# A decoder layer with a two-level Kronecker mixture of experts: the first down products spread over four quadrants, the offsets sent by a small transfer, one GELU form, and a new order of steps for all turns

## What is computed

```
n = layernorm(x)
k, v, q = fft(n Wk' + bk), fft(n Wv' + bv), fft(n Wq' + bq)
s = cumsum(k * v over the sequence) * conj(q)
x = x + real(ifft(s / (1e-9 + |s|))) / 16
x = x + cross attention(layernorm(x), ctx)         # 16 heads of 64, causal, ALiBi slopes
t = layernorm(x) seen as 64 tokens of 1024 = 32 x 32
h = gelu(kmoe(t, up)); x = x + kmoe(h, down)
kmoe: logits = t W'; top 2 of 64 experts, softmax over the two;
      out = sum over the two of p * (A[e] @ token @ B[e]')   # up 32x32 -> 64x64, down 64x64 -> 32x32
```

## Time and profile before

| | |
|---|---|
| three runs, median | 1326.86 us |
| profiled execution | 1330.54 us |
| its span, first to last instruction | 1328.8 us |
| mean granted TensorE clock | 0.981 |
| instructions | 52143 |
| start of `wo` of batch 0, 1, 14, 15 | 93.05, 161.17, 1155.58, 1232.26 us |

### The profile page before, as it was taken

The page is one execution under the profiler, slowest core; times in us unless marked ns, Lnnn a source line. Parts: engine busy times, 40 slices in busy tenths (PEclk is TensorE's granted clock), DMA queues, the critical chain, the costliest instruction groups (busy, mean ns, idle before and its releaser), DMA issues.

```text
span 1328.8 us, 52143 instructions
## 1 busy us (share of the span) xinstructions
PE 1227.9 (92%) x16626; PEld 985.8 (74%) x16626; DVE 965.7 (73%) x3677; ACT 1086.9 (82%) x3158; POOL 594.2 (45%) x1846
## 2 busy tenths in 40 slices
PE   7999999999999999999999999999999989987785
PEld 5677787877778787777778777777877777775574
DVE  1466778695978879596877969587786959777554
ACT  2557898898988899898889989798888979888654
POOL 3112446262645536363544636354553625453242
PEclk9999999999999999999999999999999999999798
DMA  9200101010110101010010101001010100101000
GB/s 287 49 17 14 38 10 42 11 42 19 30 31 13 40 14 41 16 37 24 18 39 14 42 11 41 19 19 42 11 42 12 41 19 19 34 13 32 4 25 10
DMA packets 66210, 42.58 MB, mean 32 GB/s; under 512 B 18065, under 2 KB 64786, under 8 KB 65682
## 3 DMA queue, kind: packets, MB, share of 16 engines
q1 hardware_dynamic: 65938, 39.25, 10.7%
HBM read 34.98 MB, written 4.19 MB: 29 GB/s over the span
## 4 chain that ended last, share of the span: by engine, by line
PE 54%; DVE 16%; issue 10%; SPq 10%; ACT 2%; POOL 2%; DMA 2%; DVEq 1%; POOLq 0%; ACTq 0%
SPq L483 9%; PE P L809 5%; PE X L869 5%; PE P L786 4%; PE P L775 4%; PE PT L869 4%; PE PT L832 4%; PE P L762 3%; DVE own L1142 3%; PE F L949 3%; PE X L856 3%; DVE chosen_dn L423 3%; PE S L825 2%; DVE probs L1101 2%; PE G L908 2%
## 5 line engine op out<-in xcount | busy, mean ns | idle before, releaser
L423 POOL COPY chosen_dn<-experts 64x64 f32 x1000 | 222.5, 279 | 214.2 <-issue 146.4
L664 ACT ACTIVATE probs<-probs,neg_max 128x128 f32<-128x128 f32 (+1 forms) x512 | 226.5, 444 | 24.0 <-DVE neg_max L1101 20.7
L409 POOL COPY chosen_up<-experts 32x128 f32 x512 | 182.3, 356 | 116.5 <-POOL chosen_up L409 49.7
L409 ACT COPY chosen_up<-experts 32x128 f32 x528 | 156.0, 296 | 15.5 <-PE G L955 6.2
L1101 DVE CUSTOM_DVE_ANT_0 probs<-S,distance 128x128 f32<-128x128 f32 (+1 forms) x512 | 151.9, 351 | 12.9 <-PE S L825 9.4
L832 PE MATMUL PT<-ident,probs 128*128 128x128 f32 x768 | 135.8, 286 | 10.3 <-DVE probs L1119 7.2
L703 ACT ACTIVATE hT<-h 64x1024 f32<-64x1024 f32 x64 | 127.0, 1984 | 11.3 <-DVE h L1232 9.9
L1119 DVE TENSOR_TENSOR probs<-probs,rinv 128x768 f32<-128x768 f32 x128 | 129.1, 1009 | 4.4
L775 PE MATMUL P<-ctxT,wk 128*128 128x256 f32 x512 | 124.5, 388 | 2.1 <-DVE x L1079 2.1
L786 PE MATMUL P<-wv,ctxT 128*128 128x256 f32 x512 | 122.5, 382 | 0.0
L1108 DVE COPY probsT<-PT 128x384 f32<-128x384 f32 x128 | 71.3, 557 | 70.0 <-PE PT L832 68.8
(11 more groups left out here) (133 smaller groups left out, 2855.2 us busy)
## 6 DMA issues: line engine op xcount, KB each, us to landing
chosen_up<-in_experts_up SPq DMA_DIRECT2D x992, 16.0 KB, 1.7
x<-in_x SPq DMA_DIRECT2D x16, 256.0 KB, 2.7
ctxT<-in_ctxT SPq DMA_DIRECT2D x16, 256.0 KB, 3.3
out<-x2b SPq DMA_DIRECT2D x16, 256.0 KB, 2.3
experts<-in_experts_up SPq DMA_DIRECT2D x2, 1024.0 KB, 19.8
wk<-in_xWk SPq DMA_DIRECT2D x1, 1024.0 KB
wo<-in_xWo SPq DMA_DIRECT2D x1, 1024.0 KB
wv<-in_xWv SPq DMA_DIRECT2D x1, 1024.0 KB, 7.7
```

The costliest lines, as they stand in the source:

```text
L409: last = copy(to[row:row + D1, n * 2 * F1:(n + 1) * 2 * F1], experts_up[k][:, bass.ds(held[g % loaded(units), unit], 2 * F1)])
L423: last = copy(dst, src.rearrange("p (m c) -> p m c", m=2))
L664: act.activation(probs[:, e % 4, lo:hi], probs[:, e % 4, lo:hi], ACT.Exp, bias=neg_max[:, e % 4, rt:rt + 1], scale=-1.0, accum_out=rsum[:, ...
```

## The change

- **Four quadrants.** `dn_first` alternates between the two groups of a pair: the group j = 0 goes to `F` as before, the group j = 1 to `G`, with the halves of the output crossed. For that the experts of odd groups are copied with their two matrices in different row halves, by two copies instead of one. `dn_weigh` becomes two operations, one from `F` and one from `G`. `dn_second` and `y_keep` use a bank of the `P` pair.
- **Addresses.** `place` is an integer tile of 64x2; a DMA on SP (`send_up`, `send_dn`) writes it into the row `offsets`. The diagonal and the product that spreads it hold the shares alone (128 columns). The casts are gone; the choosers load their registers from strided views.
- **One activation.** GELU is applied once, in place; then two copies on ScalarE and two on GpSimd write `hT`.
- **Order.** A new `ORDER`; 19 turns, all by it. `DRAIN`, `LAST_CHOOSERS` and `warm` are gone.

The diff, cut to its core:

```diff
-LAST_CHOOSERS = {...}
-P_USERS = ("turn1", "f", "inverse", "turn2", "k", "v", "q")
+P_USERS = ("turn1", "f", "inverse", "turn2", "k", "v", "q", "dn_second")
-G_USERS = ("logits_up", "spread_up", "up", "router_dn", "spread_dn", "dn_second", "y_turn")
+G_USERS = ("logits_up", "spread_up", "up", "router_dn", "spread_dn", "dn_first", "y_turn")
-    for turn in range(BATCH + 1):
+    last = max(lag for _, _, lag in order)
+    for turn in range(BATCH + last):
         for name, n, lag in order:
             if 0 <= turn - lag < BATCH:
                 yield name, n, turn - lag
-    for word in DRAIN.split():
...
-        SPREAD = 2 * TOKENS * TOPK
+        SPREAD = TOKENS * TOPK
...
+        def hT_parts(half, oh):
+            src = h[half * F1:(half + 1) * F1, :].rearrange("p (n h o) -> p h o n", h=2, o=F1 // 2)[:, oh]
+            return hT[oh * F1:(oh + 1) * F1, :, half * TOKENS // 2:(half + 1) * TOKENS // 2], src
...
         def choose_dn(copy, held, i, units):
-            to = chosen_dn[i % DN_SLOTS]
+            to, flip = chosen_dn[i % DN_SLOTS], i % 2
...
+                if flip:
+                    copy(to[(1 - half) * F1:(2 - half) * F1, a:a + D1], experts_dn[:, bass.ds(held[i % loaded(units), unit], D1)])
+                    last = copy(to[half * F1:(half + 1) * F1, b:b + D1],
+                                experts_dn[:, D1:][:, bass.ds(held[i % loaded(units), unit], D1)])
+                    continue
...
+            def send(c, layer):
+                groups = (UP_GROUPS, DN_GROUPS)[layer]
+                sp.wait_ge(route_step[layer], at(c, 4, 1))
+                for name in choosers_of(("up", "dn")[layer]):
+                    if name != "sync":
+                        after(sp, chosen[name][layer], at(c, groups, 0))
+                to = offsets[layer][:, :].rearrange("p (n k) -> p n k", k=TOPK)
+                sp.dma_start(to, place[layer][:, :]).then_inc(offsets_ready[layer], 16)
...
+            def turn_tokens(c):
+                after(pool, parts_done, c)
+                pool.wait_ge(h_ready, at(c, 2, 2))
+                for oh in range(2):
+                    pool.tensor_copy(*hT_parts(1, oh)).then_inc(hT_pooled, 1)
+                pool.wait_ge(hT_pooled, at(c, 2, 2))
...
             def gelu(c):
                 wait_g(act, "up", UP_PAIRS, c)
-                after(act, parts_done, c)
-                for half in range(2):
-                    for oh in range(2):
...
-                        act.activation(dst, src, ACT.Gelu).then_inc(hT_ready, 1)
                 cols = UP_PAIRS // 2 * UP_TOK * F1
-                act.wait_ge(hT_ready, at(c, 4, 4))
                 for i in range(2):
                     part = slice(i * cols, (i + 1) * cols)
                     act.activation(h[:, part], h[:, part], ACT.Gelu).then_inc(h_ready, 1)
+            def turn_tokens(c):
+                after(act, parts_done, c)
+                act.wait_ge(h_ready, at(c, 2, 2))
+                for oh in range(2):
+                    act.copy(*hT_parts(0, oh)).then_inc(hT_ready, 1)
...
-                pe.matmul(G[:, 128:384], route_ones[:, :], route_diag[layer][:, :], start=True, stop=True).then_inc(route_spread[layer], 1)
+                pe.matmul(G[:, 128:256], route_ones[:, :], route_diag[layer][:, :], start=True, stop=True).then_inc(route_spread[layer], 1)
...
-                for j in (0, 1):
-                    g, slot = i + j * DN_PAIRS, (2 * i + j) % DN_SLOTS
-                    for u in range(DN_TOK // 2):
+                for u in range(DN_TOK // 2):
+                    for j in (0, 1):
+                        g, slot = i + j * DN_PAIRS, (2 * i + j) % DN_SLOTS
+                        token, one = g * UP_TOK + u, slice((j * 4 + u) * w, (j * 4 + u + 1) * w)
                         for half in range(2):
-                            rows = slice(half * F1, (half + 1) * F1)
-                            token = g * UP_TOK + u
-                            mm = pe.matmul(F[rows, (j * 4 + u) * w:(j * 4 + u + 1) * w], h[rows, token * F1:(token + 1) * F1],
+                            rows, to = [slice(e * F1, (e + 1) * F1) for e in (half, half ^ j)]
+                            mm = pe.matmul((F, G)[j][to, one], h[rows, token * F1:(token + 1) * F1],
...
-                dve.tensor_tensor(W_dn[:, :].rearrange("p (s w) -> p s w", w=D1),
-                                  F[:, :].rearrange("p (s w) -> p s w", w=D1),
-                                  spread(pm[1][:, i * n:(i + 1) * n], 2, D1), ALU.mult).then_inc(f_kept, 1)
+                for j, (bank, kept) in enumerate(((F, f_kept), (G, g_kept))):
+                    part, by = slice(j * n * F1 // 4, (j + 1) * n * F1 // 4), slice(i * n + j * n // 2, i * n + (j + 1) * n // 2)
+                    dve.tensor_tensor(W_dn[:, part].rearrange("p (s w) -> p s w", w=D1),
...
```

More of the change, by code:

```diff
@@ L85 @@
-scale.0@1 gap_up@2 q_keep.2@1 turn1 choose_dve.18@3 weights_up@2 turn_a.0@1 choose_act.17@3 score.1@1 q_keep.3@1
-catch_a.0@1 dn_first.0@3 turn_b.0@1 mask.1@1 choose_act.18@3 choose_act.19@3 spread_up@2 v.0@1 dn_weigh.0@3 keep_up@2
-choose_sync.0@2 xnT1 dn_second.0@3 exp.1@1 catch_b.0@1 choose_dve.19@3 score.2@1 dn_first.1@3 v_keep.0@1 scale.1@1
-pv.0@1 y_keep.0@3 mask.2@1 dn_weigh.1@3 choose_sync.1@2 choose_sync.2@2 choose_act.0@2 choose_sync.3@2
-choose_pool.20@3 choose_act.20@3 choose_act.21@3 choose_act.1@2 turn_a.1@1 choose_dve.20@3 f.0 dn_second.1@3
@@ L90 @@
-choose_act.2@2 score.3@1 exp.2@1 choose_act.3@2 choose_dve.21@3 choose_pool.21@3 dn_first.2@3 y_keep.1@3
-choose_dve.22@3 scale.2@1 dn_weigh.2@3 catch_a.1@1 f_keep.0 keep_out.0@1 choose_pool.22@3 choose_act.4@2
-choose_act.22@3 choose_dve.23@3 f.1 turn_b.1@1 catch_b.1@1 mask.3@1 choose_sync.4@2 choose_sync.5@2 choose_sync.6@2
-choose_sync.7@2 f_keep.1 v.1@1 turn_a.2@1 pv.1@1 choose_pool.23@3 dn_second.2@3 choose_act.23@3 choose_pool.0@2
-own_dve@2 exp.3@1 dn_first.3@3 score.4@1 y_keep.2@3 catch_a.2@1 turn_b.2@1 catch_b.2@1 dn_weigh.3@3 keep_out.1@1
@@ L95 @@
-v_keep.1@1 v.2@1 scale.3@1 dn_second.3@3 pv.2@1 choose_pool.1@2 turn_a.3@1 y_keep.3@3 mask.4@1 choose_pool.2@2
-y_turn@3 choose_pool.3@2 own_act@2 choose_pool.4@2 final@3 store@3 choose_pool.5@2 v_keep.2@1 catch_a.3@1 exp.4@1
-v.3@1 turn_b.3@1 cross.0 product_kv keep_out.2@1 lane.0 up.0@2 catch_b.3@1 weigh.0@2 score.5@1 up.1@2 choose_act.5@2
-choose_act.6@2 choose_act.7@2 scale.4@1 mask.5@1
-"""
-DRAIN = """
-pre.0@14 pv.3@15 turn_a.4@15 catch_a.4@15 keep_out.3@15 weigh.1@14 turn_b.4@15 catch_b.4@15 score.6@15 mask.6@15
@@ L142 @@
[L142 to L158 removed]
+choose_pool.3@3 choose_pool.4@3 k.1@1 spread_up@3 turn_b.3@2 keep_up@3 up.0@3 mask.5@2 weigh.0@3 k_keep.1@1
@@ new lines @@
+weigh.6@3 turn_a.7@2 catch_a.7@2 mask.0@1 q.2@1 pre.5@3 turn_b.7@2 choose_sync.15@3 up.7@3 catch_b.7@2 pv.7@2 pre.6@3
+weigh.7@3 ln1_root ln1 q_keep.1@1 score.1@1 up.8@3 exp.0@1 keep_out.7@2 pre.7@3 gelu@3 hT_pool@3 wo.0@2 wo.1@2
+hT_act@3 router_dn@3 logits_dn.0@3 mask.1@1 q_keep.2@1 scale.0@1 exp.1@1 x2.0@2 x2.1@2 ln3_stats@2 ln3_root@2
+x1_bias@1 logits_dn.1@3 logits_dn.2@3 logits_dn.3@3 part@3 fold@3 top_dn@3 send_dn@3 choose_pool.16@3 ln3@2 gap_dn@3
+v.1@1 scale.1@1 weights_dn@3 q.3@1 v_keep.1@1 choose_dve.16@3 turn_a.0@1 spread_dn@3 ln3_turn@2 choose_dve.17@3
@@ new lines @@
+keep_dn@3 choose_pool.17@3 choose_act.16@3 catch_a.0@1 ln3_keep@2 turn1 turn_b.0@1 choose_pool.18@3 catch_b.0@1
+choose_dve.18@3 score.2@1 mask.2@1 logits_up@2 pv.0@1 top_up@2 own_dve@2 choose_dve.19@3 send_up@2 xnT1 q_keep.3@1
+choose_act.17@3 exp.2@1 turn_a.1@1 v.2@1 v_keep.2@1 dn_first.0@3 choose_act.18@3 choose_pool.19@3 keep_out.0@1
+catch_a.1@1 f.0 f.1 turn_b.1@1 choose_act.0@2 f_keep.0 dn_weigh.0@3 scale.2@1 catch_b.1@1 choose_act.19@3
+dn_second.0@3 choose_pool.20@3 f_keep.1 dn_first.1@3 score.3@1 choose_act.20@3 gap_up@2 choose_act.1@2 dn_weigh.1@3
@@ new lines @@
+pv.1@1 dn_second.1@3 choose_sync.0@2 choose_sync.1@2 choose_pool.21@3 choose_pool.22@3 y_keep.0@3 choose_act.2@2
+choose_dve.20@3 turn_a.2@1 f.2 choose_act.3@2 choose_act.21@3 choose_sync.2@2 y_keep.1@3 choose_act.4@2 f_keep.2
+choose_dve.21@3 mask.3@1 choose_dve.22@3 v.3@1 catch_a.2@1 exp.3@1 choose_pool.23@3 cross.0 dn_first.2@3 score.4@1
+choose_sync.3@2 product_kv lane.0 turn_b.2@1 k.3@1 v_keep.3@1 dn_weigh.2@3 keep_out.1@1 choose_dve.23@3 catch_b.2@1
+mask.4@1 load_ctx dn_second.2@3 choose_act.22@3 choose_act.23@3 pv.2@1 k_keep.3@1 dn_first.3@3 score.5@1 scale.3@1
@@ L978, in dn_second @@
             def dn_second(c, i):
-                take_g("dn_second", i, c)
+                bank = take_p("dn_second", i, c)
                 wait_f(pe, "dn_first", i, c)
+                wait_g(pe, "dn_first", i, c)
                 for odd in (0, 1):
```

219 lines of the change are left out of this document (76 added, 143 removed).

## The result

The changed kernel takes **1447.1 us** (median of four runs, 1444.8 to 1448.3), the kernel before 1326.4 on the same chip. The ratio is **1.091 (1.089 to 1.093)**: 121 us slower, where 10 us less were forecast. The profiled execution's span is 1446.5 us against 1328.8.

A forecast was written before the change was run, and what follows sets the result against it. TensorE's own work was taken to bound the steady turns, a chain of dependent steps the last two stretches. Turns -22, start +5, before the last wo -9, behind it +16 gave -10 on 1328.8, carried over to 1316 us; range 1297 to 1340.

The forecast's parts named there:

- Part 1(a): Odd down groups: one 64x64 copy becomes two; GpSimd half copy 0.15 us, odd group 2.4 (1.5 to 3.0), off TensorE.
- Part 2: Offsets by small transfer: spreading products save 0.5 us a batch, transfer takes 2.0, GpSimd's doubled down-offset loads 2 x 0.57.
- Part 3: One GELU, then strided copies, 2.6 us each on GpSimd: TensorE waits 1.7 us a turn at the router (0.2 to 3.9).
- rival 1: The router's wait on TensorE isn't absorbed: a turn becomes 77.1 us, total 1347, slower; chance 0.24.
- Part 1: Four-quadrant first down products: a dn_first step falls from 1.04 to 0.63 us, saving 1.6 us a batch on TensorE.
- Rival 3: In dn_first the four quadrants don't overlap: the saving falls to 0.5 us a turn, total 1340; chance 0.04.
- Part 4: The steady turn between wo starts: from 76.5 to 74.8 us (73.4 to 77.9), -22 us over 13 turns.
- Part 5: Both ends: start +5 us, before the last wo -9, behind the last wo +16 (8 to 24).

The follow-up runs named there:

- a1: The changed kernel with odd groups' copies made one row half after the other instead of alternating, four quadrants kept: 1358.7 us, ratio 1.028.
- b5: The kernel before with odd down groups chosen by two 64x32 copies into the same row half, nothing crossed: 1364.1 us, ratio 1.027.
- a5: The changed kernel with odd groups' copies made one row half after the other and up offsets packed side by side: 1341.7 us, ratio 1.011.
- a4: The changed kernel with the crossing undone (first down products in two quadrants) and up offsets packed side by side: 1339.4 us, ratio 1.013.
- a2: The changed kernel with GpSimd's and ScalarE's up offsets sent again, packed so that register loads read eight neighbouring values: 1426.1 us, ratio 1.079.
- b3: The kernel before with its steady order run for 19 turns, without written-out end, last-batch shares and filler products: 1344.2 us, ratio 1.012.

## Why the prediction was wrong

**The step that failed first: Part 1(a), the price of a half copy.** I took 0.15 us, from the elements, and bounded an odd group by 1.5 and 3.0 us. A half copy that changes the row half costs 0.25 us on GpSimd, an odd group 4.0, outside my bounds. I scaled a row of another pattern: the eight copies of the earlier trace rows all write the same rows. I laid this cost off TensorE, so in the sum for the turn it stood at nothing; TensorE waited 50 us for these copies over the 13 turns, and their order was worth 5.8 us a turn (a1).

**The same step also lacked cover.** I wrote that the price lies off TensorE and let it lie beside other work. In the earlier trace rows `dn_first` starts without a wait, and I didn't ask how much slack the copies had before the product needed them. The rows had the answer: GpSimd's second group ends at 565.06 and the product starts at 565.85. Over the turns the last copy ended 0.8, 0.5, 0.8 and 1.9 us (medians) before the four products of a batch, while each odd group grew by 2.5 us. b5 gives the price in the old order, 2.1 us a turn for the added copies even at the cheap rate, the larger part of it not in `dn_first` but in what VectorE makes behind its copies. In the new order a5 against a4 shows the same in small: TensorE saves 1.7 us and the turn 0.2.

**Part 2, the loads.** I counted the down loads' doubling (2 x 0.57, the median of a row in which up and down loads are mixed; measured 4 x 1.08 in place of two of 2.0) and missed the up loads altogether. Offsets laid out by the small transfer put gaps between the pairs, and a load goes from 0.57 to 1.88 us. It is worth 1.5 us a turn (a2). The transfer itself lands in 1.7 us at the median; I had taken 2.0. The transfer has landed before `choose_dve.16`, as I said. But VectorE is idle there 1.16 us in each turn, for its two loads of 0.6 us each, where it was mostly 0.49. `keep_dn` stands behind it, and the up router waits for `keep_dn`: 12.0 us over the 13 turns (line 866 above), where it waited 1.0.

**Part 3 and rival 1, the router's wait: not there.** One copy on GpSimd takes 1.95 us; I took 2.6, about the middle between 2.0 and 3.4, and 0.5 for interference. The strided ScalarE row was the right neighbour and the two-operand row the wrong one. The bounds of the wait, 0.2 and 3.9, don't follow from 2.0 and 3.4 either: with the stated terms they are 0 (without interference) and 3.3, and 0 is what came. ScalarE's strided copy takes 2.0 us, as its strided GELU did. (The rule on throughput that I drew from the Trainium skill, "ScalarE: Activation LUTs", stands there under "Step-by-step: what each stage is for".) The Trainium skill, "GPSIMD Engine Reference" (7. Performance pitfalls for Q7 kernels), states about 2.9 cycles an element for strided reads, which gives 2.5 us here, an estimate; the trace disagrees, 1.95 us, and the measurement decides. Rival 1 said slower, and slower it is, but by another wait: its price was 8 us in the turns and its place was the router. A rival about the copies was missing, since I had bounded them too tightly.

**Part 1, the products: right, and better.** A `dn_first` step runs from 610.41 to the next step's start at 610.90, 0.49 us; I took 0.63 where it was 1.04. The step's first line stands in the section on the result; these are its last line and the next step:

```profile
610.89 0.22 PE L945 MATMUL G<-chosen_dn,h 64*64 64x64 f32 x2
610.90 0.43 PE L792 MATMUL S<-kT,qT 64*64 64x128 f32 x8
```

It is the four quadrants and not the second bank: a4, which writes both banks from two quadrants, takes 1.08 us from its first product to the next step.

```profile
640.46 0.33 PE L953 MATMUL F<-chosen_dn,h 64*64 64x64 f32 x4
...
641.54 3.72 PE L740 MATMUL P<-xnT,wf 128*128 128x256 f32 x16
```

Four such steps save 2.2 us a batch, and TensorE's busy time with the copies grouped (a5) is 71.6 us a turn after 73.5. Rival 3 falls. The bracket in the step's first line shows what took the saving: 1.37 us of waiting, in one step of four.

**Part 4, the turn.** Forecast 74.8, measured 82.8. Of the 8.0 us, the alternation is 5.8 (a1), the strided up loads 1.2 to 1.5 (a5 against a1, a2 against the changed kernel), and about 1.0 stays when both are gone (a5, 75.8): there TensorE is idle 4.2 us a turn, where it was 3.0 before.

**Part 5, the ends.** Start +5: right. Behind the last `wo`: the old order with the common end gives +19 for +16 (b3), in the pieces that I had named, so the mechanism was right; the changed kernel shows +31. The last `pre` starts 76.5 us behind `wo` where I had 70 (`store` of batch 14 is issued at 49 instead of 43), and from the last `place` to the end it takes 39 us where I had 29. With the crossing gone and loads packed (a4) these are 68 and 32. Before the last `wo` I forecast 68; a1, a4 and a5 show 72 to 73. The work moved out of that turn was less than the 9 us I took off; that size is off in every variant.

**Small slips in the sums.** The median 1326.9 less 10 is 1317, not 1316, and the last `pre` before the change starts 59.1 us behind `wo` by the earlier trace rows, where I wrote 59.5. Neither matters beside the 121 us.

## What to carry to other kernels

Splitting one copy into two to save TensorE time has to be priced from a row in which the copies go in the same order over the same partitions; where two targets alternate, group them by target, which cost nothing here and gave 5.8 us of an 82.8 us turn. Before a cost is called hidden, look for how long the consumer could wait: a group with no idle time before it says only that the producer is in time, not by how much. Look also at what else the same engine makes behind the added work. When the layout of a small table changes, look at every reader, register loads too.
